# GpSimd scales and shifts the entropy model's input, ScalarE takes both sides' tanh at once

## The reference, cut to what matters

```python
def _logits_cumulative(logits, ms, bs, fs):
    for i in range(4):
        logits = einsum('cij,cjn->cin', softplus(ms[i]), logits) + bs[i]
        if i < 3:
            logits = logits + tanh(fs[i]) * tanh(logits)
    return logits
lower = _logits_cumulative(xr - 0.5, ms, bs, fs)
upper = _logits_cumulative(xr + 0.5, ms, bs, fs)
sign = -jnp.sign(lower + upper)
likelihood = maximum(abs(sigmoid(sign * upper) - sigmoid(sign * lower)), 1e-6)
...
x = x + attention(_gn(x))
x = x + likelihood(_gn(x))
```

## Time and profile before

| | |
|---|---|
| median of 3 runs | 4755.69 us (4754.44 to 4764.46) |
| profiled execution | 4754.35 us, span 4752.5 us |
| PE, DVE, ACT, POOL busy | 93%, 86%, 79%, 17% of the span |
| first tanh L792, 128x1024 | x368, mean 1251 ns |
| first tanh L792, 48x1024 | x32, mean 1237 ns |
| layer tanh L799 | x768, mean 1120 ns |
| gate L1123 | x768, mean 1277 ns |

### The profile page before, as it was taken

One profiled execution on the slowest core, in us unless ns is written; L12 is line 12 of the kernel. 1 busy time (PEld: TensorE's weight loads), 2 busy tenths in 40 slices (PEclk: granted clock), 3 DMA queues, 4 the chain that ended last, 5 costly groups with the idle time before them and its releaser, 6 DMA issues.

```text
span 4752.5 us, 108300 instructions
## 1 busy us (share of the span) xinstructions
PE 4428.2 (93%) x38780; PEld 2977.4 (63%) x38780; DVE 4099.3 (86%) x5433; ACT 3736.5 (79%) x4214; POOL 813.8 (17%) x937
## 2 busy tenths in 40 slices
PE   5999989999899999999899998999989999899976
PEld 3888338873488735887258862688617885278821
DVE  6997899978999789996999969999698987999866
ACT  2777788868888698886988869787797877978787
POOL 4100201202022110211111120121201212022112
PEclk9999999999999999999999999999999999999998
DMA  2000321114211142111411124110331112311133
GB/s 68 25 21 25 97 73 53 38 39 100 68 51 36 44 103 62 46 44 40 111 51 53 36 58 104 40 61 28 78 89 49 47 41 75 93 49 34 40 93 94
DMA packets 155019, 280.19 MB, mean 59 GB/s; under 512 B 37441, under 2 KB 37921, under 8 KB 152706
## 3 DMA queue, kind: packets, MB, share of 16 engines
q1 hardware_dynamic: 154434, 272.69, 21.4%
HBM read 205.24 MB, written 50.33 MB: 54 GB/s over the span
## 4 chain that ended last, share of the span: by engine, by line
PE 72%; ACT 11%; DVE 7%; issue 7%; DMA 0%; ACTq 0%; POOL 0%; DVEq 0%; POOLq 0%
PE ps L1514 14%; PE ps L1512 14%; PE ps L1516 13%; PE ps L1288 9%; PE ps L1465 8%; ACT th L799 5%; ACT arena L792 4%; PE ps L1387 3%; PE ps L1321 3%; DVE th L1123 3%; PE ps L1373 3%; PE ps L1345 2%; DVE mxp L1191 2%; PE ps L1296 1%; PE ps L1280 1%
## 5 line engine op out<-in xcount | busy, mean ns | idle before, releaser
L1514 PE MATMUL ps<-v_sb,arena 128*128 128x192 f16 x8192 | 2026.8, 247 | 0.0
L1512 PE MATMUL ps<-v_sb,arena 128*128 128x193 f16 x8192 | 2017.9, 246 | 0.0
L1516 PE MATMUL ps<-v_sb,arena 128*128 128x193 f16 x8192 | 2009.9, 245 | 0.0
L755 ACT ACTIVATE arena<-ps 128x1024 f16<-128x1024 f32 x1024 | 1049.0, 1024 | 644.5 <-PE ps L1288 640.7
L1083 DVE TENSOR_TENSOR arena<-ps,arena 128x1024 f16<-128x1024 f32 x1024 | 1245.6, 1217 | 166.8 <-ACT ps L756 158.5
L1191 DVE TENSOR_REDUCE mxp<-ps 128x1 f32<-128x512 f32 x1792 | 1191.0, 688 | 41.3 <-PE ps L1465 29.3
L1123 DVE SCALAR_TENSOR_TENSOR th<-th,gates,ps 128x1024 f32<-128x1024 f32 x768 | 950.3, 1277 | 147.2 <-ACT th L799 140.1
L756 ACT ACTIVATE ps<-ps 128x1024 f32<-128x1024 f32 x1024 | 1044.4, 1020 | 0.0
L1514 PEld LDWEIGHTS ps<-v_sb,arena 128*128 128x128 f16 x8192 | 795.1, 97 | 262.7 <-issue 0.6
L799 ACT ACTIVATE th<-ps,biases 128x1024 f32<-128x1024 f32 x768 | 825.6, 1120 | 118.5 <-PE ps L1373 80.8
L1512 PEld LDWEIGHTS ps<-v_sb,arena 128*128 128x128 f16 x8192 | 792.1, 97 | 126.3 <-issue 10.8
(11 more groups left out here) (147 smaller groups left out, 3449.8 us busy)
## 6 DMA issues: line engine op xcount, KB each, us to landing
x<-x2d SPq DMA_DIRECT2D x1152, 64.0 KB, 2.3
arena<-x2d SPq DMA_DIRECT2D x768, 64.0 KB, 2.5
xp<-x_dram SPq DMA_DIRECT2D x18, 1536.0 KB, 10.1
shared<-x_dram SPq DMA_DIRECT2D x64, 384.0 KB, 3.9
x2d<-shared SPq DMA_DIRECT2D x64, 384.0 KB, 3.0
res<-x2d SPq DMA_DIRECT2D x96, 256.0 KB
out_dram<-res SPq DMA_DIRECT2D x96, 256.0 KB
kst<-shared SPq DMA_DIRECT2D x32, 256.0 KB, 3.2
```

What stands on the lines that cost most here:

```text
L755: act.activation(e_hi[:, q % 4, :].rearrange("p (k n) -> p k n", k=2), sc, ACT.Exp)
L1512: pe.matmul(acc, eh, v_sb[:, m, 0:C + 1], start=(m == 0 and t % 2 == 0), stop=False, skip_group_check=True)
L1514: pe.matmul(acc[:, 0:C], eh, v_sb[:, m, VW:VW + C], start=False, stop=False, skip_group_check=True)
L1516: ins = pe.matmul(acc, el, v_sb[:, m, 0:C + 1], start=False, stop=(m == MT - 1), skip_group_check=True)
```

## The change

For the first two halves (v = 0, 1, `DIRECT` = 2) the first tanhs stay as they are. For v = 2 to 23 GpSimd computes `scl * x4 + biases[d]` into `t0` for both sides (two tensor_scalar instructions of 128x1024, `shift`), and ScalarE takes one tanh in place over both sides (128x2048, no scale or bias operand, `first_tanhs`). `shift(2)` stands behind `root2` on GpSimd, ahead of `queries(2)`; the others at even slots, v = s / 2 + 3, ahead of the tail's operations of that slot. `first_tanhs(v)` stands at the end of odd slots, v = (s + 3) / 2; even slots have none. The wait for `t0`'s last reader (`h1_mm`) and for `x4` moves from ScalarE to GpSimd. On SyncE `load_x4(v + 3)` now waits for the shift of v (`pre_ready`) and stands ahead of `load_side(v)`.

```diff
                     for v in range(HALVES):
+                        if v + X4R < HALVES:
+                            if v < DIRECT:
+                                read = sp.compute_val(l * SLOTS + 2 * v + 2)
+                                settle(sp)
+                                sp.wait_ge(t0_ready, read)
+                            else:
+                                shifted_on = sp.compute_val(l * 2 * (HALVES - DIRECT) + 2 * (v - DIRECT) + 2)
+                                settle(sp)
+                                sp.wait_ge(pre_ready, shifted_on)
+                            load_x4(row, v + X4R)
                         if v >= SPLIT:
                             load_side(l, row, v)
-                        elif v + X4R < HALVES:
-                            read = sp.compute_val(l * SLOTS + 2 * v + 2)
-                            settle(sp)
-                            sp.wait_ge(t0_ready, read)
-                        if v + X4R < HALVES:
-                            load_x4(row, v + X4R)
...
+                def shift(v):
+
+                    u = v // 2
+                    pool.wait_ge(x4_in[v % X4R], l * (HALVES // X4R) * X4_DMAS * 16 + X4_DMAS * 16 * (v // X4R + 1))
+                    if v == DIRECT:
+                        normed = pool.compute_val(l * GN2_STEPS + 16)
+                        settle(pool)
+                        pool.wait_ge(gn2_step, normed)
+                    if v >= T0R:
+                        mixed = pool.compute_val(l * SLOTS + 2 * (v - T0R) + 2)
+                        settle(pool)
+                        pool.wait_ge(h1_mm, mixed)
+                    for d in range(2):
+                        pool.tensor_scalar(t0[:, v % T0R, d, :], x4[:, v % X4R, :], scl[:, u:u + 1],
+                                           biases[:, d, 0, u:u + 1], ALU.mult, ALU.add).then_inc(pre_ready, 1)
+
                 if proj:
                     queries(0)
                     queries(1)
                 root2(l)
+                shift(DIRECT)
...
                 for s in range(SLOTS + 6):
                     if proj and s >= 1 and s - 1 + V_LEAD < VB:
                         values(s - 1 + V_LEAD)
+                    if s % 2 == 0 and s // 2 + DIRECT + 1 < HALVES:
+                        shift(s // 2 + DIRECT + 1)
...
                     if d == 0:
                         act.wait_ge(x4_in[v % X4R], l * (HALVES // X4R) * X4_DMAS * 16 + X4_DMAS * 16 * (v // X4R + 1))
-                        if v >= T0R:
-                            act.wait_ge(h1_mm, l * SLOTS + 2 * (v - T0R) + 2)
...
+                def first_tanhs(v):
+
+                    shifted_on = act.compute_val(l * 2 * (HALVES - DIRECT) + 2 * (v - DIRECT) + 2)
+                    settle(act)
+                    act.wait_ge(pre_ready, shifted_on)
+                    act.activation(t0[:, v % T0R, :, :], t0[:, v % T0R, :, :], ACT.Tanh).then_inc(t0_ready, 2)
...
-                for i in range(LEAD):
+                for i in range(2 * DIRECT):
                     first_tanh(i)
...
-                    if s + LEAD < SLOTS:
-                        first_tanh(s + LEAD)
+                    if s % 2 == 1 and s + LEAD - 1 < SLOTS:
+                        first_tanhs((s + LEAD - 1) // 2)
```

More of the change, by code:

```diff
@@ L55 @@
 LEAD = 4
+DIRECT = 2
 SPLIT = 1
@@ L311, in program @@
         x4_in = [sem(f"x4_in{s}") for s in range(X4R)]
+        pre_ready = sem("pre_ready")
         t0_ready = sem("t0_ready")
```

## The result

The changed kernel takes 4776.58 us (median of 7 runs, 4774.47 to 4779.58) against 4757.24 before (7 runs): ratio 1.004, 95% interval 1.0028 to 1.0052, so slower by 0.4%. The forecast was 4764 with slower as the likeliest sign; the profiled execution took 4776.89 against 4754.35, +22.5 us where the sum had said +10.

What follows compares the result with a forecast made beforehand. VectorE was taken as the fullest engine in seven images' entropy slots 12 to 43, ScalarE in the last image. Terms +20 (slots 12 to 43), -10 (last image) and 0 on 4754.35 gave 4764 us; range 4726 to 4802.

Steps and rivals of the forecast that it cites:

- The main term: Entropy slots 12 to 43: period 13.90 us in place of 13.54, +0.36 for 8 periods in 7 images, +20.2 us.
- My chain: Seven steps from slot 4's gate to slot 8's, 13.90 us a period; chance 0.60, own range 4754 to 4776.
- Wide tanh, shift, GpSimd hidden: ScalarE's wide tanh takes 1.896 us, GpSimd's shift operation 1.2; GpSimd's work is hidden behind the loop.
- The slope behind 1.896: ScalarE's tanh price: 1.042 us for 1024 and 0.615 for 512 give 0.834 ns an element, 1.896 us for 2048.
- Slots 12 to 43: Entropy stage, seven images: third layers 13.90 us apart instead of 13.54, VectorE idle some 0.6 a period, +20.2 us.
- the rival of VectorE alone: Layer-two wait in the odd slot doesn't appear, VectorE runs through: 13.25 us a period, 4728 in all; chance 0.17.
- Heads and slots 0 to 11: Early entropy slots with the value projection, TensorE full: 0 us taken, bounds -5 to +8.
- The last image: Entropy stage without maxima, ScalarE fullest: period 14.3 us instead of 15.36, -1.05 for 10 periods, -10 us in all.
- Cost 0: SyncE's queue: x4 loads wait for the shift and stand ahead of the side loads, at no cost.
- well ahead of slot 2: SyncE's side loads for v=1 stand behind six more issues but still come in time for slot 2.
- the forecast's 0.4 of waits: Last image: about 0.4 us of wait a period on the third layer's way, part of the 14.3 period.
- Contention: Rival: each of a shift's two GpSimd operations holds one VectorE gate by 0.4 us, +45 more, 4809; chance 0.10.

Runs made afterwards that it cites:

- e2: Changed kernel with shift kept, but one narrow tanh a slot again, each with two pointer operands; 4761.02 us, ratio to before 1.0006.
- e1: Changed kernel with shift kept, but one narrow tanh (128x1024, no pointers) in every slot instead of a wide one per pair; 4733.13 us, ratio to before 0.995.
- e5: Changed kernel with two pointer operands on the wide tanhs of slots 1, 5, 9 ... (slots with logits), some 0.19 us longer each; 4777.33 us.
- e6: Changed kernel with two pointer operands on the wide tanhs of slots 3, 7, 11 ... instead; 4785.81 us, ratio to before 1.0059.
- e7: Changed kernel with each image's first shift (v = 2) waiting for w1s instead of the step that writes the biases; 4777.25 us, ratio to before 1.0044.
- e4: Changed kernel with the side loads of v = 1 ahead of the x4 loads of v = 4 on SyncE; 4773.88 us, ratio to before 1.0033.
- e8: Changed kernel with narrow tanhs in seven images, wide in the last's odd slots, v = 1 side loads earlier, first shift behind w1s; 4731.79 us.

## Why the prediction was right, and where it was not

The time lies in the stated range and the sign is the likeliest one, but the change is about twice the forecast's: +22.5 us for a sum of +10.2. The main term was right in cause and size. The missing 12.3 us are terms that the forecast had at nothing, too low, or not at all: +4.3 in heads and early slots, +4.3 in the last image, +5.0 at the changeover, +1.7 in the rest of the attention, and 2.8 too much for slots 12 to 43. My chain's own range ended at 4776, just under the median of 4776.58.

- **Wide tanh, shift, GpSimd hidden:** right; 1.905 and 1.212 us against 1.896 and 1.2, and e2 shows the shift with next to no cost in slots 12 to 43. The slope behind 1.896 was taken from two rows that the forecast both calls tanhs; the one of 512 (L770) is `size`, an abs. It held for the tanh all the same.
- **Slots 12 to 43:** right, by mechanism and size. 13.86 for a forecast of 13.90; +17.4 us measured over seven images, forecast +20.2. e1 (13.24, VectorE through), e5 and e6 (one of two tanhs is in the cycle) show the mechanism; the rival of VectorE alone was the e1 kernel, and its 13.25 was right for that.
- **Heads and slots 0 to 11:** the term "I take 0, bounds -5 to +8" measured +4.3, and all of it lies in the heads (slots 0 to 5, +4.5), where the even-odd order costs half a microsecond an image (e2 and e7) and a longer wide tanh of slot 1 costs its 0.18 (e5). In slots 5 to 13 TensorE isn't alone in setting the pace either: from the first third layer to the second it takes 15.85 for 15.61, and e6 lengthens that by 0.18. The next period is 0.14 shorter at a granted clock of 1.00 (16.42 to 16.28), and some 1.0 longer at 0.90, which three images have after the change and four before. So the -0.2 of this stretch holds a microsecond of the clock.
- **The last image:** forecast -10, measured -5.7. Two steps failed. "Cost 0" for SyncE's queue: the side loads of v = 1 come behind six more x4 loads, and there the first layer of slot 2 waited 2.84 us; "well ahead of slot 2" holds only in images where the projection stands between. And the period came out at 14.57 instead of 14.3: one of the tail's tanhs waits for GpSimd's sum, which the forecast's 0.4 of waits left out. In the changed kernel's trace it waits 0.34 us (`L787`, released by L590). That this is all of the difference wasn't tried.
- **The changeover to the attention (+5.0)** had no term at all. It goes with TensorE's clock, below; whether the change makes the slow case more frequent stays open.
- **Contention:** the gates were rightly left alone, their mean is 1.275 us (1.277 before). But the rule of the Trainium skill that I cited ("SBUF — State Buffer", "Who interferes with whom") speaks of any VectorE instruction with two SBUF inputs, and I had checked the gates only. w1s is such a one and took 0.88 us more, in each image. By that rule it should, and the trace agrees; its cost in time is nothing (e7).

## What to carry to other kernels

In a loop of in-order engines, count what stands between a result and the operation that needs it on the busiest queue before you merge two operations: two short ones, one a step, covered a latency of 3.8 us that one long one in every second step lays bare. Two operations can be made a fifth cheaper together (2.26 us to 1.80) and the loop still get slower; find the cycle of operations that wait for each other, and see how many of the merged operations it holds. Keep the cheaper price and the even spacing apart: here dropping the pointers was worth 28 us (4761 to 4733), and merging cost 43 (4733 to 4776).

## What was not expected of the hardware

TensorE's clock falls at the changeover to the attention in some images and not in others. The gap from the eleventh to the twelfth third layer takes 15.4, some 16.5 or some 17.7 us. Busy time over this gap (columns: stretch, its length, busy us and count of PE, PEld, DVE, ACT, POOL, then granted clock, DMA share, GB/s), first and second image before the change:

```profile
666.76:683.35 16.59, 12.76 (x90) 5.41 (x89) 13.52 (x13) 10.95 (x12) 0.47 (x1) 0.90 0.59 138
1245.85:1261.25 15.40, 11.29 (x89) 4.15 (x89) 12.98 (x13) 10.94 (x12) 0.00 (x0) 1.00 0.59 134
```

and the first image after it, the whole gap and its first 3 us:

```profile
669.69:687.44 17.75, 14.08 (x90) 5.68 (x89) 13.68 (x13) 10.87 (x12) 0.38 (x1) 0.81 0.56 126
...
669.00:672.00 3.00, 2.42 (x13) 0.75 (x17) 2.80 (x5) 0.70 (x1) 0.00 (x0) 0.58 0.02 5
```

A granted share of 0.58 means that most of these 3 us ran at the lower of the two levels, 1.2 instead of 2.4 GHz; the third layer there took 3.48 us instead of 1.92 (TensorE had waited 1.11 us ahead of it). Over the ten traces, 70 gaps, length and clock go together without an exception: the 19 gaps of 15.4 have a granted clock of 1.00, the 41 of 16.4 to 16.7 have 0.90, the 10 of 17.6 to 17.9 have 0.81 or 0.82. Before the change three images of seven have 15.4 and none 17.7; after it none has 15.4 and one 17.7. That is all of the +5.0. But e4, e5, e6 and e7, with the same order of tanhs, have one, two, four and one images of 15.4, and the narrow kernels e1 and e8 have one of 17.7 each, so seven images of one profiled run are too few to blame the change for the 5 us.

The second point is how the two engines share in the contention above. The first pair of shifts of the changed kernel, and w1s:

```profile
488.02 1.21 POOL L664 TENSOR_SCALAR arena<-x,scl,biases 128x1024 f32<-128x1024 f32 x1 [4.04 <-DVE biases L1041]
488.19 1.84 DVE L1046 TENSOR_TENSOR w1s<-w,rowscale 128x768 f32<-128x768 f32 x1
489.23 1.88 POOL L664 TENSOR_SCALAR arena<-x,scl,biases 128x1024 f32<-128x1024 f32 x1
```

The first shift takes its usual 1.21. w1s starts 0.17 us behind it and ends 0.80 after it; the second shift ends 1.07 after w1s. So each held up the one that had started behind it, in all eight images. With the shift behind w1s (e7) the same happens one step later: the first shift takes 1.19, a VectorE product with two SBUF inputs that starts beside it 1.06 instead of 0.75, and the second shift 1.62, so the pair takes 2.80 us where an undisturbed one takes 2.37.
